# Edge network of a graph kernel: block parts copied one step later, and four groups' sums gathered in one PSUM bank

## The chip, the cores and the metric

The kernel runs on one core of one Trainium2 chip. The metric is the device time of one execution, in microseconds. Engines are named as in the profile: PE (TensorE; PEld is its weight loading), DVE (VectorE), ACT (ScalarE), POOL (GpSimd) and SP (SyncE, which here only issues transfers).

## The reference

12,500 nodes with 96 features, 400,000 edges sorted by destination, 32 attributes an edge. The edge network, the part that the change touches, computes for each edge a message and a gate and sums their products by destination:

```python
edge_input = jnp.concatenate([x[src], edge_attr], axis=-1)
messages = _gelu(edge_input @ mW1 + mb1) @ mW2 + mb2
gates = jax.nn.sigmoid(_gelu(edge_input @ gW1 + gb1) @ gW2 + gb2)
aggregated = jax.ops.segment_sum(messages * gates, dst, num_segments=x.shape[0])
combined = jnp.concatenate([x, aggregated], axis=-1)
update = _gelu(combined @ uW1 + ub1) @ uW2 + ub2
```

A layer norm follows, and then two graph convolutions, each a sum over the same edges weighted by edge weight and degrees, with a gated mix of old and new features:

```python
msg = norm[:, None] * h[row]
out = jax.ops.segment_sum(msg, col, num_segments=n)
g = jax.nn.sigmoid(h_in @ Wr + br)
x = jax.nn.relu((1.0 - g) * h_in + g * xc)
```

## The kernel before, in words

The edges lie in tiles of 128. Four tiles are a quad, two quads a group, two groups (four quads, 2,048 edges) an iteration of the edge network; there are 196 iterations and 392 groups. `edge_pass` runs them on every engine in step: 4 iterations that prepare (`prepare`), then 192 that also build (`pair`, two iterations in a loop body). Each engine follows its own written order, and semaphores couple them. The four steps s = 0 to 3 of an iteration are the four quads:

- POOL (`gather`) fetches the source rows of a quad with four indirect transfers into `hid[s]`, as soon as the quad four places earlier has been weighed (`s_gated`). An iteration needs 16 gathers.
- PE (`edges`) at step s multiplies the attributes of the quad three places ahead (`attr_product`), builds block part 2s (`build_part`, twelve bf16 matmuls into one of the three banks of `part_bank`), waits for the quad's weighed messages and sums them by destination with four matmuls (L1149), and builds part 2s + 1.
- DVE (`edges`) at step s makes the one-hot matrix and the gate column (`gate`), adds a finished window of sums to `acc` (`window_sum`, at s = 0 and s = 2), makes one-hot operands for the block parts (`spread_sides`, L1700 to L1703), multiplies and reduces the gate's logits of the next quad (`dot`), and adds attributes to gathered rows two quads ahead (`add`).
- ACT (`edges`) at step s weighs the messages of the quad by the gate (`weigh`, L1352, four activations, after which `s_gated` rises), copies part 2s from PSUM to `blocks` (`keep_part`, L1361), does the tanh of the next quad and the gelu of the one after it, and copies part 2s + 1.

A group's sums cover 64 destinations (`WINDOW`), in columns of bank `sg[0]`, one half for each of the iteration's two groups. `window_sum` reads the group's first destination from `base_i` and adds 98 rows by 64 columns to `acc` there; it waits for PE's sums of the group's second quad (`s_seg`), and PE starts the next sums of that half only after it (`s_acc`). `hot` and `msg` have two buffers each, so `gate` of a quad waits for PE's sums of the quad two before. The block parts take three banks in turn: `build_part(i)` waits until the part that was in its bank has been copied (`bank_free`, `s_evac`). `spread_sides` at s = 2 overwrites operands of parts 0 to 3 and waits until part 3 is built; at s = 0 it does so for parts 4 to 7 of the iteration before.

The blocks, adjacency matrices of the last 1,536 tiles, go to DRAM and feed the convolutions, whose code the change leaves alone.

Of the kernel before, what the change touches and what calls it, by code (L numbers as in the profile page):

```python
# [20 lines left out]
I32 = mybir.dt.int32  # L21
# [3 lines left out]
AX = mybir.AxisListType  # L25
# [26 lines left out]
ACC = NODES + WINDOW  # L52
# [6 lines left out]
SETUP_STEPS = 21  # L59
# [112 lines left out]
def build(nc, io):  # L172
    ctx = contextlib.ExitStack()
    with ctx:
# [34 lines left out]
        with contextlib.ExitStack() as edges_phase:  # L209
# [8 lines left out]
            iota_z = sb_in(edges_phase, "iota_z", [P, 2 * Z_PAD], F16)  # L218
        table_sb = sb("table_sb", [P, BLOCKS * D])
# [149 lines left out]
        sums = [sg[0][:, WINDOW * g:WINDOW * (g + 1)] for g in range(GROUPS_PER_ITER)]  # L369
# [207 lines left out]
        def edge_pass(eng, rounds, iteration, round_end=None, part=None, round_start=None, alone=0, end=None):  # L577
# [3 lines left out]
            with eng.Fori(0, rounds) as r:  # L581
                n0 = eng.snap(r * ITERS)
                o0 = eng.snap(r * OCTETS)
                w0 = eng.snap(r * OCTET_PAIRS)

                def prepare(c, ahead):
                    done = eng.snap(r * SLICES + c)
                    if part:
                        part(c, done)
                    iteration(c, n0 + c, isinstance(c, int) and c == 0, False, None, ahead)  # L590
                    if end:
                        end(c, done)

                def pair(w, final):
                    for h in range(2):
# [4 lines left out]
                                  None if last else (o + 1, eng.snap(o0 + o + 1)))  # L600
# [3 lines left out]
                prepare(0, None)  # L604
                with eng.Fori(1, SLICES - 1) as c:
                    prepare(c, None)
                prepare(SLICES - 1, (0, o0))
# [42 lines left out]
        def _(sp):  # L650
# [47 lines left out]
            def edges(it, n, first, last, build, ahead):  # L698
# [205 lines left out]
        def _(pool):  # L904
# [43 lines left out]
            def gather(it, n, first, last, build, ahead):  # L948
# [12 lines left out]
            def gather_end(r):  # L961
                wait_apart(pool, s_acc, r * GROUPS + GROUPS)
# [75 lines left out]
        def _(pe):  # L1038
# [64 lines left out]

            def load_places(nb):
# [26 lines left out]
            def edges(it, n, first, last, build, ahead):  # L1131
# [6 lines left out]
                for s in range(QUADS_PER_ITER):  # L1138
# [7 lines left out]
                    if s % 2 == 0 and not (first and s == 0):  # L1146
                        pe.wait_ge(s_acc, GROUPS_PER_ITER * n + s // 2)
# [8 lines left out]
            def edges_end(r):  # L1156
                pe.wait_ge(s_acc, r * GROUPS + GROUPS)
# [131 lines left out]
        def _(act):  # L1289
# [65 lines left out]
            def keep_part(i, nb, h, w):  # L1355
                q, b = divmod(i, QUAD_PARTS)
# [9 lines left out]
            def edges(it, n, first, last, build, ahead):  # L1366
# [4 lines left out]
                for s in range(QUADS_PER_ITER):  # L1371
                    weigh(n, s)
                    if build:
                        keep_part(2 * s, *build[1:])
# [8 lines left out]
                    if build:  # L1383
                        keep_part(2 * s + 1, *build[1:])
# [17 lines left out]
            edge_pass(act, rounds, edges, lambda r: act.wait_ge(s_acc, r * GROUPS + GROUPS),  # L1402
# [102 lines left out]
        def _(dve):  # L1505
# [76 lines left out]
            do.did(v.tensor_scalar(top[:, 1:2], top[:, 0:1], 0.0, None, ALU.max))  # L1582
# [15 lines left out]

            def add_window(it, n, g, rows, first, s_sum, value, s_done):

                start = dve.value_load(base_i[0:1, bass.ds(it * GROUPS_PER_ITER + g, 1)], min_val=0, max_val=NODES)
                window = acc[0:rows, bass.ds(start, WINDOW)]
                if not first:
                    dve.wait_ge(s_done, GROUPS_PER_ITER * n + g)
                dve.wait_ge(s_sum, value)
                v.tensor_tensor(window, window, sums[g][0:rows, :], ALU.add).then_inc(s_done, 1)  # L1606
# [101 lines left out]
            def window_sum(it, n, g, first):  # L1708
                add_window(it, n, g, ACC_ROWS, first, s_seg, QUADS_PER_ITER * n + 2 * g + 2, s_acc)
# [438 lines left out]
```

## Time and profile before

| | |
|---|---|
| median of 3 runs | 10818.27 us (10817.15 to 10834.14) |
| profiled execution, its own time | 10833.28 us |
| its span | 10831.3 us |
| edge network, first to last add to `acc` | 163.5 to 5712.1 us |
| what follows it (node update, two convolutions) | to the span's end |

The profiled execution lies 15 us above the median, and 2 us of its time lie outside the span. Lines of a timeline give the start in us, the duration in us, the engine, the line of the kernel, the operation with output and inputs, how many instructions the line merges (x8), and in brackets the idle time of the engine before it with what ended it. "remote" there is a semaphore whose raiser the profile does not name. The starts and ends of matmuls are PE's own records and their ends are modelled; when another engine gets to see a matmul's semaphore can only be read from that engine's own row.

### The profile page before, as it was taken

The page shows a single profiled execution, that of the slowest core. Times are in us where ns is not written, and L with a number is a line of the kernel's source. Part 1 is how long each engine was busy: PE and PEld are TensorE (multiplying, and loading weights), DVE is VectorE, ACT ScalarE, POOL GpSimd, SP SyncE. Part 2 cuts the span into 40 slices and gives each one's busy share as a digit, 9 for nine tenths or more (in the row PEclk, how much of TensorE's full clock was granted, in tenths as well). Part 3 has the DMA queues.
Part 4 walks back from the last instruction along what each step waited for, and adds up shares of the span by engine and source line. Part 5 has one row for each costly group of instructions (what it writes and reads, how often), then busy time and mean ns, then how long its engine had stood idle before and what let it go on. Part 6 is the DMA issues. An engine that isn't in the chain of part 4 may idle for free. (4 is left out here: it accounts for less than half of the span.)

```text
span 10831.3 us, 151063 instructions
## 1 busy us (share of the span) xinstructions
PE 8115.2 (75%) x42144; PEld 5216.6 (48%) x42144; DVE 4910.5 (45%) x11836; ACT 2686.7 (25%) x6600; POOL 6404.8 (59%) x6424
## 2 busy tenths in 40 slices
PE   4777777777777777777777577787777578877876
PEld 3555555555555555555554333343334333333333
DVE  7666666666666666666666122222222122222222
ACT  3444444444444444444443000000000000000000
POOL 4555555555555555555555666666664666666664
PEclk7888888888888888888887788888887688888887
DMA  4444444444444444444444466666665466665656
GB/s 148 128 137 137 134 140 132 139 132 139 132 138 135 136 138 133 139 132 139 131 139 152 144 212 215 207 228 209 211 214 200 157 208 223 216 220 200 222 207 213
DMA packets 936184, 1818.04 MB, mean 168 GB/s; under 512 B 280495, under 2 KB 748736, under 8 KB 878448
## 3 DMA queue, kind: packets, MB, share of 16 engines
q10 hardware_dynamic: 65600, 773.65, 18.9%
q1 hardware_dynamic: 618592, 578.41, 16.9%
q0 software_dynamic: 251856, 464.10, 16.1%
q8 instruction: 93, 1.52, 0.1%
q14 instruction: 43, 0.35, 0.0%
HBM read 1361.12 MB, written 454.48 MB: 168 GB/s over the span
## 5 line engine op out<-in xcount | busy, mean ns | idle before, releaser
L956 POOL DMA_INDIRECT hid<-src_table,src_ids x3127 | 3121.3, 998 | 2450.0 <-ACT msg L1352 1514.8
L1234 PE MATMUL bd<-ring,table_sb 128*96 128x480 f32 x6272 | 2898.5, 610 | 382.7 <-issue 381.5
L1234 PEld LDWEIGHTS bd<-ring,table_sb 128*96 128x96 f32 x6272 | 1070.0, 175 | 1954.7 <-issue 1954.7
L1001 POOL DMA_INDIRECT hid<-conv_table,hid x1596 | 1552.2, 973 | 715.1 <-issue 488.4
L1149 PE MATMUL sg<-hot,msg 128*98 128x64 f32 x6272 | 817.2, 283 | 1256.1 <-ACT msg L1352 1256.1
L1149 PEld LDWEIGHTS sg<-hot,msg 128*98 128x98 f32 x6272 | 733.3, 196 | 1379.3 <-issue 1303.6
L1001 POOL DMA_INDIRECT feat_in<-conv_table,hid x1056 | 1022.6, 968 | 588.6 <-issue 342.8
L1126 PE MATMUL bd<-one_hot_dst,one_hot_src 128*128 128x168 bf16 (+1 forms) x10368 | 1246.2, 275 | 88.5 <-issue 87.6
L1966 DVE TENSOR_TENSOR acc<-acc,sg 96x64 f32 x400 | 87.3, 218 | 2365.6 <-remote 1368.1
L1361 ACT ACTIVATE blocks<-bd 128x480 f32<-128x480 f32 (+1 forms) x1152 | 657.8, 571 | 1971.7 <-PE bd L1126 941.6
L1126 PEld LDWEIGHTS bd<-one_hot_dst,one_hot_src 128*128 128x128 bf16 x10368 | 1013.5, 110 | 108.6 <-issue 94.3
L1703 DVE SCALAR_TENSOR_TENSOR one_hot_src<-iota_lo,side_now 128x384 bf16<-128x384 bf16 x1536 | 933.0, 607 | 0.0
L1352 ACT ACTIVATE msg<-hid,msg 128x96 f32<-128x96 f32 x3136 | 909.8, 363 | 46.5 <-DVE msg L1680 46.5
L1093 PE MATMUL pa<-w_attr,attr 128*128 128x384 f32 x1568 | 815.5, 656 | 57.1 <-DVE hid L1656 26.9
L1606 DVE TENSOR_TENSOR acc<-acc,sg 98x64 f32 x392 | 86.9, 222 | 1430.5 <-remote 1363.5
L1459 ACT ACTIVATE buf_b<-pa,mix_b_half 96x448 f32<-96x448 f32 x56 | 35.2, 629 | 2817.9 <-PE pa L1243 1635.9
L1339 ACT ACTIVATE hid<-hid 128x768 f32<-128x768 f32 x784 | 656.9, 838 | 279.1 <-DVE hid L1656 223.9
L1001 POOL DMA_INDIRECT rows_more<-conv_table,hid x528 | 525.0, 994 | 293.5 <-issue 157.3
L1093 PE MATMUL pb<-w_attr,attr 128*128 128x384 f32 x1568 | 596.4, 503 | 9.0 <-issue 9.0
L1944 DVE TENSOR_TENSOR conv_hot<-iota_now,hid 128x512 f32<-128x512 f32 x134 | 92.5, 691 | 1019.7 <-remote 581.9
L1093 PEld LDWEIGHTS pa<-w_attr,attr 128*128 128x128 f32 x1568 | 394.6, 279 | 263.6 <-issue 160.5
L1473 ACT ACTIVATE hid<-bd,side_flag 96x480 f32<-96x480 f32 x32 | 21.0, 657 | 1884.6 <-PE bd L1234 893.4
(248 smaller groups left out, 10323.9 us busy)
## 6 DMA issues: line engine op xcount, KB each, us to landing
ring<-adjacency ACTq DMA_DIRECT2D x448, 1680.0 KB
adjacency<-blocks SPq DMA_DIRECT2D x384, 980.0 KB
attr<-in_attr SPq DMA_DIRECT2D x392, 128.0 KB
hid<-src_table,src_ids POOLq DMA_INDIRECT x3127
hid<-conv_table,hid POOLq DMA_INDIRECT x1596
feat_in<-conv_table,hid POOLq DMA_INDIRECT x1056
conv_table<-table_sb SPq DMA_DIRECT2D x28, 336.0 KB, 2.5
feat_half<-feat_keep SPq DMA_DIRECT2D x56, 168.0 KB
```

Source lines behind the costliest of these rows:

```text
L956: pool.indirect_dma_start(out=hid[s][:, t, :], out_offset=None, in_=src_rows, in_offset=bass.IndirectOffsetOnAxis(ap=src_ids[s // 2][:, j: ...
L1001: pool.indirect_dma_start(out=conv_g[j][slot][:, t, :], out_offset=None, in_=conv_rows[l], in_offset=bass.IndirectOffsetOnAxis(ap=conv_ids ...
L1093: last = nc.tensor.matmul(attr_ps[s % 2][:, 512 * h:512 * h + 2 * H2], attr[s // 2][:, P * (s % 2):P * (s % 2 + 1)], w_attr[:, 2 * H2 * h: ...
L1126: op = nc.tensor.matmul(out[:, :, bass.ds(places[q][t], FAN)], y_s[q][t][:, k, :], z_s[q][t][:, z0:z0 + FAN * m].rearrange("p (b d) -> p b ...
L1149: op = nc.tensor.matmul(sums[s // 2][0:ACC_ROWS, :], msg[s % 2][:, t, :], hot[s % 2][:, t, :], start=(s % 2 == 0 and t == 0), stop=(s % 2 ...
L1234: op = nc.tensor.matmul(side_ps[w].rearrange("r (o z) -> r o z", o=UNIT_OCTETS), table_sb[:, D * k:D * (k + 1)], ring[slot][:, :, OCTET_FA ...
L1339: nc.scalar.activation(flat, flat, ACT.Gelu).then_inc(s_gelu, 1)
L1352: op = nc.scalar.activation(m[:, t, 0:D], hid[s][:, t, 0:D], ACT.Copy, scale=m[:, t, GATE_ROW:GATE_ROW + 1])
L1361: nc.scalar.activation(blocks[h][:, first:first + m, WIDTH * q:WIDTH * (q + 1)], part_bank[i % BANKS][:, 0:WIDTH * m].rearrange("p (b w) - ...
L1703: v.scalar_tensor_tensor(out=y_s[q][t][:, :, :], in0=iota_lo[:, :].unsqueeze(1).to_broadcast([P, 3, P]), scalar=side_now[:, 0, QUAD * q + ...
L1944: v.tensor_tensor(conv_s[j][slot], iota_now[:, :].unsqueeze(1).to_broadcast([P, GROUP, WINDOW]), conv_rel[j][:, cols].unsqueeze(2).to_broa ...
L1966: v.tensor_tensor(window, window, sg[j][0:D, WINDOW * slot:WINDOW * (slot + 1)], ALU.add).then_inc(s["acc"], 1)
```

## The change

It has two parts.

**Copies a step later (ACT).** `keep_part` at step s copies parts 2s - 2 and 2s - 1 in place of 2s and 2s + 1; at s = 0 these are the last two parts of the iteration before. Banks, waits of PE and sizes stay.

**One sum for four groups (PE, DVE).** Two iterations (four groups) form a span. A span has a first destination (`span_base`), each group an offset in it of 0 to 96 (`offset_i`), limited there, with what exceeds it taken into the group's own positions. PE reads the two offsets of an iteration into registers, clears 160 columns of `sg[0]` at the start of a span with one matmul of zeros after DVE has added the span before, and lets all 32 matmuls of the span add at their register offset. DVE adds 98 by 160 to `acc` once a span (`span_sum`), at s = 0 of the next span's first iteration, behind `add`. The two `window_sum` of each iteration go. The preparing iterations are written out instead of looped, and the setup has seven more small DVE steps on 128 by 392 values.

```diff
+                if half == 0 and s == 0:
+                    if not first:
+                        pe.wait_ge(s_acc, span)
+                    nc.tensor.matmul(sums, zero[:, :].to_broadcast([P, ACC_ROWS]), first_base[:, 0:SPAN], start=True, stop=False)
                     for t in range(QUAD):
-                        op = nc.tensor.matmul(sums[s // 2][0:ACC_ROWS, :], msg[s % 2][:, t, :],
-                                              hot[s % 2][:, t, :], start=(s % 2 == 0 and t == 0),
-                                              stop=(s % 2 == 1 and t == QUAD - 1))
+                        op = nc.tensor.matmul(sg[0][0:ACC_ROWS, bass.ds(offset[s // 2], WINDOW)], msg[s % 2][:, t, :],
+                                              hot[s % 2][:, t, :], start=False,
+                                              stop=(half == SPAN_ITERS - 1 and s == QUADS_PER_ITER - 1 and t == QUAD - 1))
...
                 for s in range(QUADS_PER_ITER):
                     weigh(n, s)
-                    if build:
-                        keep_part(2 * s, *build[1:])
+                    behind = build and not (s == 0 and isinstance(build[0], int) and build[0] == 0)
+                    if behind:
+                        keep_part(2 * s - 2, *build[1:])
                     if s + 1 < QUADS_PER_ITER:
                         tanh(n, s + 1, not (first and s == 0))
...
-                    if build:
-                        keep_part(2 * s + 1, *build[1:])
+                    if behind:
+                        keep_part(2 * s - 1, *build[1:])
+                if last:
+                    for i in (PARTS - 2, PARTS - 1):
+                        keep_part(i, *build[1:])
...
-            def window_sum(it, n, g, first):
-                add_window(it, n, g, ACC_ROWS, first, s_seg, QUADS_PER_ITER * n + 2 * g + 2, s_acc)
-
-            def edges(it, n, first, last, build, ahead):
+            def span_sum(it, n, span):
+
+                start = dve.value_load(span_i[0:1, bass.ds(it // SPAN_ITERS, 1)], min_val=0, max_val=N)
+                total = acc[0:ACC_ROWS, bass.ds(start, SPAN)]
+                after(dve, s_acc, span)
+                dve.wait_ge(s_seg, QUADS_PER_ITER * (n + SPAN_ITERS))
+                v.tensor_tensor(total, total, sums, ALU.add).then_inc(s_acc, 1)
...
                     gate(it, n, s, not (first and s < 2))
-                    if s == 0 and not first:
-                        window_sum(it - 1, n - 1, 1, False)
-                    if s == 2:
-                        window_sum(it, n, 0, first)
...
+                    if s == 0 and half == 0 and not first:
+                        span_sum(it - SPAN_ITERS, n - SPAN_ITERS, span - 1)
                 if last:
-                    window_sum(it, n, 1, False)
+                    span_sum(it - (SPAN_ITERS - 1), n - (SPAN_ITERS - 1), span)
...
+            def load_offsets(it):
+                _, offsets = nc.values_load_multi_w_load_instructions(
+                    offset_i[0:1, bass.ds(it * GROUPS_PER_ITER, GROUPS_PER_ITER)], engines=[mybir.EngineType.PE],
+                    min_val=0, max_val=LAST_OFFSET, skip_runtime_bounds_check_because="DVE has bounded them")
+                return offsets
```

The order of instructions at three places shows it. First ACT, step 0 of a building iteration, before:

```order
L1352 ACTIVATE msg<-hid,msg 128x96 [waits gate_columns]
L1352 ACTIVATE msg<-hid,msg 128x96 x3
L1358 ISA
L1359 ISA [waits blocks_kept0]
L1361 ACTIVATE blocks<-bd 128x24x20 [waits block_built]
L1342 REGISTER_ALU
L1345 ACTIVATE buf_h<-buf_h,gate_b_half 128x4 [waits gated,gate_logits]
L1337 REGISTER_ALU
L1339 ACTIVATE hid<-hid 128x768 [waits added]
```

and the same place now:

```order
L1370 ACTIVATE msg<-hid,msg 128x96 [waits gate_columns]
L1370 ACTIVATE msg<-hid,msg 128x96 x3
L1380 ISA
L1382 ACTIVATE blocks<-bd 128x24x20 [waits block_built]
L1360 REGISTER_ALU
L1363 ACTIVATE buf_h<-buf_h,gate_b_half 128x4 [waits gated,gate_logits]
L1355 REGISTER_ALU
L1357 ACTIVATE hid<-hid 128x768 [waits added]
```

The rows read alike, but the copy (L1361, now L1382) behind the weighing is that of part 6 of the iteration before, where it was part 0 of this one; the wait for the stored blocks has moved on with part 0 to step 1. Next DVE at the start of an iteration that is the first of its span, from the gate to the operands of the block parts, before:

```order
L1678 COPY msg<-weight 128x4
L1679 REGISTER_ALU
L1680 TENSOR_SCALAR msg<-buf_h 128x4 [waits tanh_done]
L1601 ISA
L1601 TENSOR_LOAD base_i
L1601 ISA x2
L1604 ISA
L1605 ISA [waits accumulated]
L1606 ISA [waits segment_sums]
L1606 TENSOR_TENSOR acc<-acc,sg 98x64
L1696 ISA
L1700 TENSOR_SCALAR one_hot_wide<-iota_wide,side_now 128x1960 [waits block_built]
```

and now, from the end of the same gate to the add to `acc`:

```order
L1712 TENSOR_SCALAR msg<-buf_h 128x4 [waits tanh_done]
L1728 ISA
L1732 TENSOR_SCALAR one_hot_wide<-iota_wide,side_now 128x1960 [waits block_built]
...
L1697 TENSOR_TENSOR prod<-hid,gate_w 128x384 [waits gate_logits,gelu_done]
L1700 TENSOR_REDUCE buf_h<-prod 128x4 [waits gate_products]
L1685 ISA
L1686 REGISTER_ALU [waits gathered2]
L1688 TENSOR_TENSOR hid<-pa,hid 128x768 [waits attr_product]
L1742 ISA
L1742 TENSOR_LOAD span_i
L1742 ISA x2
L145 ISA
L1746 ISA [waits segment_sums,accumulated]
L1746 TENSOR_TENSOR acc<-acc,sg 98x160
```

The wait for PE's sums (`segment_sums`) no longer stands between the gate and the operands; the operands' own wait for the parts (`block_built`, L1700, now L1732) is the next one there. Last PE at the sums of the same step, before:

```order
L1126 MATMUL bd<-one_hot_dst,one_hot_src 128x24x7 x3
L1145 REGISTER_ALU
L1147 REGISTER_ALU [waits gated]
L1149 MATMUL sg<-hot,msg 98x64 [waits accumulated]
L1149 MATMUL sg<-hot,msg 98x64 x3
L1115 REGISTER_ALU
L1120 MATMUL bd<-one_hot_wide,one_hot_src 128x500 [waits block_copied]
```

and now:

```order
L1141 MATMUL bd<-one_hot_dst,one_hot_src 128x24x7 x3
L1161 REGISTER_ALU
L1164 REGISTER_ALU [waits gated]
L1165 MATMUL sg<-first_base,zero 98x160 [waits accumulated]
L1167 ISA
L1167 MATMUL sg<-hot,msg 98x64 x4
L1130 REGISTER_ALU
L1135 MATMUL bd<-one_hot_wide,one_hot_src 128x500 [waits block_copied]
```

The wait for DVE's add has moved to the matmul of zeros, which stands there in every second iteration; at the other steps the sums wait for the weighing alone.

## Rows read from the trace of the kernel before

**Rows 1.** Edge network as one stretch: busy PE, PEld, DVE, ACT, POOL, granted clock, DMA

```profile
330.00:5720.00 5390.00, 4088.61 (x27394) 3119.51 (x27392) 3438.55 (x8549) 2414.32 (x6089) 3022.66 (x3031) 0.86 0.45 136
```

**Rows 2.** The line L1606, all of the program

```profile
L1606 DVE TENSOR_TENSOR acc<-acc,sg x392: 207/222/225, 163.5 to 5712.1; 98x64 f32 x196
```

**Rows 3.** Who waited for whom, 600 to 5600 us: total, times, longest

```profile
DVE acc L1606 <- remote: 1274.8, 329, 5.3
...
PE sg L1149 <- ACT msg L1352: 1110.0, 352, 5.9
ACT blocks L1361 <- PE bd L1126: 888.2, 337, 5.1
ACT blocks L1361 <- remote: 799.5, 178, 6.2
```

**Rows 4.** Timeline of one half iteration, 3033.9 to 3047.9 us

```profile
3033.95 0.90 PE L1149 MATMUL sg<-hot,msg 128*98 128x64 f32 x8 [2.14 <-ACT msg L1352]
...
3034.62 1.05 POOL L956 DMA_INDIRECT hid<-src_table,src_ids  x1 [3.72 <-ACT msg L1352]
...
3038.13 0.99 PE L1126 MATMUL sg<-one_hot_dst,one_hot_src 128*128 128x168 bf16 x9
...
3038.95 0.84 PE L1149 MATMUL sg<-hot,msg 128*98 128x64 f32 x8
...
3039.16 0.57 ACT L1361 ACTIVATE blocks<-sg 128x480 f32<-128x480 f32 x1 [0.44 <-PE sg L1126]
...
3040.01 1.02 PE L1126 MATMUL bd<-one_hot_dst,one_hot_src 128*128 128x175 bf16 x9
...
3043.79 0.94 POOL L956 DMA_INDIRECT hid<-src_table,src_ids  x1 [0.30 <-issue]
3044.81 0.22 DVE L1606 TENSOR_TENSOR acc<-acc,sg 98x64 f32 x1 [3.72 <-remote]
3046.16 0.59 ACT L1361 ACTIVATE blocks<-bd 128x500 f32<-128x500 f32 x1 [4.90 <-remote]
3046.16 0.73 DVE L1700 TENSOR_SCALAR one_hot_wide<-iota_wide,side_now 128x1960 bf16<-128x1960 f16 x1 [1.13 <-remote]
...
3047.93 1.59 PE L1149 MATMUL sg<-hot,msg 128*98 128x64 f32 x8 [4.41 <-ACT msg L1352]
```

**Rows 5.** Two half iterations side by side, busy time and granted clock

```profile
3019.90:3032.10 12.20, 11.90 (x72) 8.94 (x72) 7.08 (x18) 4.59 (x11) 8.13 (x8) 0.75 0.27 75
3033.90:3046.10 12.20, 9.30 (x72) 7.13 (x72) 7.34 (x21) 4.64 (x11) 7.98 (x8) 1.00 0.75 240
```

**Rows 6.** Groups of instructions, 600 to 5600 us: busy, mean ns, idle before

```profile
L956 POOL DMA_INDIRECT hid<-src_table,src_ids x2823 | 2815.8, 997 | 2182.2 <-ACT msg L1352 1364.0 <-issue 818.2
...
L1703 DVE SCALAR_TENSOR_TENSOR one_hot_src<-iota_lo,side_now 128x384 bf16<-128x384 bf16 x1411 | 857.0, 607 | 0.0
...
L1352 ACT ACTIVATE msg<-hid,msg 128x96 f32<-128x96 f32 x2824 | 819.3, 363 | 0.0
...
L1361 ACT ACTIVATE blocks<-bd 128x500 f32<-128x500 f32 (+1 forms) x1059 | 604.7, 571 | 1799.3 <-PE bd L1126 872.2 <-remote 789.3 <-issue 137.1
L1339 ACT ACTIVATE hid<-hid 128x768 f32<-128x768 f32 x706 | 591.6, 838 | 205.1 <-DVE hid L1656 204.2 <-issue 0.4
...
L1702 DVE TENSOR_SCALAR one_hot_dst<-iota_z,side_now 128x688 bf16<-128x688 f16 x1059 | 422.3, 399 | 0.0
...
L1668 DVE TENSOR_REDUCE buf_h<-prod 128x4 f32<-128x384 f32 x705 | 389.9, 553 | 24.2
L1665 DVE TENSOR_TENSOR prod<-hid,gate_w 128x384 f32<-128x384 f32 x705 | 386.4, 548 | 0.0
...
L1656 DVE TENSOR_TENSOR hid<-pa,hid 128x768 f32<-128x768 f32 x352 | 333.6, 948 | 0.0
L1676 DVE TENSOR_TENSOR hot<-iota_now,rel 128x256 f32<-128x256 f32 x705 | 291.3, 413 | 0.0
```

**Rows 7.** Register load of the block places, PE's sequencer, all of the program

```profile
L1106 PEldq TENSOR_LOAD <-side_off x192: 813/817/850, 272.3 to 5690.7; - x192
```

More of the change, by code:

```diff
@@ L51 @@
 WINDOW_LOG2 = 6
-ACC = NODES + WINDOW
+SPAN_ITERS = 2
+SPANS = ITERS // SPAN_ITERS
+SPAN_GROUPS = GROUPS // SPANS
+LAST_OFFSET = 96
+SPAN = LAST_OFFSET + WINDOW
+ACC = N + SPAN
 GATE_ROW = D
@@ L368, in build @@
         iota, gate_w2_now = iota_now[:, :], gate_w2[:, :]
-        sums = [sg[0][:, WINDOW * g:WINDOW * (g + 1)] for g in range(GROUPS_PER_ITER)]
+        sums = sg[0][0:ACC_ROWS, 0:SPAN]
         part_bank = [px, const, sg[1]]
@@ L589, in prepare @@
                         part(c, done)
-                    iteration(c, n0 + c, isinstance(c, int) and c == 0, False, None, ahead)
+                    iteration(c, n0 + c, c == 0, False, None, ahead, c % SPAN_ITERS, s0 + c // SPAN_ITERS)
                     if end:
@@ L599, in pair @@
                         iteration(it, n0 + it, False, last, (o, eng.snap(o0 + o), h, eng.snap(w0 + w)),
-                                  None if last else (o + 1, eng.snap(o0 + o + 1)))
+                                  None if last else (o + 1, eng.snap(o0 + o + 1)), h,
+                                  eng.snap(s0 + w + BUILD_FROM // SPAN_ITERS))
                 if round_start:
                     round_start(r)
[L604 to L607, printed above, removed]
+                for c in range(SLICES):
+                    prepare(c, (0, o0) if c == SLICES - 1 else None)
                 for w in range(alone):
@@ L696, in store_blocks, with edges @@
                              kept[:, i, :, :]).then_inc(s_block_out[h], 16)
-            def edges(it, n, first, last, build, ahead):
+            def edges(it, n, first, last, build, ahead, half, span):
                 for b in range(GROUPS_PER_ITER):
@@ L946, in _, with gather @@
                 pool.wait_ge(s_table_out[p], 16 * (CHUNKS // 2))
-            def gather(it, n, first, last, build, ahead):
+            def gather(it, n, first, last, build, ahead, half, span):
                 for s in range(QUADS_PER_ITER):
@@ L1129, in build_part, with edges @@
                 op.then_inc(s_built, 1)
-            def edges(it, n, first, last, build, ahead):
+            def edges(it, n, first, last, build, ahead, half, span):
+                offset = load_offsets(it)
                 if build:
@@ L1364, in keep_part, with edges @@
                     ACT.Copy).then_inc(s_evac, 1)
-            def edges(it, n, first, last, build, ahead):
+            def edges(it, n, first, last, build, ahead, half, span):
                 if first:
@@ L1597, in _ @@
             new_source(CHUNKS - 1, (CHUNKS - 1) % 2)
[L1599 to L1606, printed above, removed]
             def place_windows(do, slots, shift, flag):
@@ L1706, in spread_sides, with edges @@
                                            op0=ALU.is_equal, op1=ALU.mult).then_inc(s_yz, 1)
-            def window_sum(it, n, g, first):
-                add_window(it, n, g, ACC_ROWS, first, s_seg, QUADS_PER_ITER * n + 2 * g + 2, s_acc)
-            def edges(it, n, first, last, build, ahead):
+            def span_sum(it, n, span):
[4 more added lines that the diff above has]
+                v.tensor_tensor(total, total, sums, ALU.add).then_inc(s_acc, 1)
+            def edges(it, n, first, last, build, ahead, half, span):
                 if first:
```

43 lines of the change are left out of this document (35 added, 8 removed).

## The prediction

> **What bounds the kernel now.** I read the busy shares first. Over 5,390 us of the edge network no engine is full: PE 76%, DVE 64%, POOL 56%, ACT 45% [rows 1]. So something makes them take turns. From the first to the last add to `acc` 5548.6 us pass [rows 2], 28.3 us for each of 196 iterations. The groups of instructions give POOL's share of that: a gather takes 997 ns, and with the issue gaps (818.2 us over 2,823) one starts each 1.29 us [rows 6], 20.6 us for sixteen. POOL is idle the other 7.7 us, for the weighing of messages: in the same row of [rows 6] 1364.0 us are put down to ACT. The chain of waits would name two lines as guilty, DVE's add to `acc` (1274.8 us, 329 times) and ACT's copies of block parts (888.2 + 799.5 us), while PE's sums wait 1110.0 us for ACT [rows 3].
>
> The timeline shows what stands behind them. In the half iteration of [rows 4] PE sums a quad at 3033.95, POOL starts eight gathers at 3034.62 and starts the last at 3043.79. PE's sums of the second quad are recorded as ended at 3039.79 (3038.95 + 0.84), yet the DVE add that waits for them starts at 3044.81. Block part 3 ends at 3041.03 in PE's record, yet ACT's copy and DVE's L1700 that wait for it both start at 3046.16. Then come the copy, the weighing (L1352) and PE's next sums at 3047.93. Early in the run of gathers it is otherwise: the part that ends at 3039.12 is copied from 3039.16. So a matmul's end is seen at once in about the first 5 us of a run of gathers, and after that only when the run is over, here 2.4 us after the last gather started. I can't say why; I only take the rule. PE's own speed doesn't set it: one half iteration with 11.90 us of PE work at clock 0.75, and the next with 9.30 us at 1.00, are both 14 us long [rows 5].
>
> A half iteration then adds up to 0.7 (sums to first gather) + 7 x 1.29 + 2.4 (release) + 0.6 (copy) + 1.2 (four times 363 ns [rows 6]) = 13.9 us. Two make 27.8 where 28.3 are measured, so the sum is 2% short. The engines stop for each other twice an iteration.
>
> **The span sums.** The 392 adds of 222 ns [rows 2] go, 87 us of DVE's time; 98 adds of 160 columns come. Their price lies between the 0.22 of 64 columns and the 0.55 of a 384-column operation [rows 6]; I take 0.32, so 31 us. Both lie in DVE's slack, and count only in a chain through DVE. But the wait of this add isn't worth its 1,275 us: behind it stands L1700 with its own wait for part 3, and in [rows 4] that costs 1.13 us more. Gone alone, the first wait becomes the second, at the same moment. PE's 98 matmuls of zeros are each about one sum of the `sg` kind (0.11 us in [rows 4], 0.90 for eight) up to 0.4: at most 40 us, behind POOL's stop, so nothing. PE also loads two offsets an iteration: one load of the block places takes 0.82 us [rows 7], so 196 x 0.82 = 160 us if it stood in the open. It stands at the head of an iteration, ahead of a product that PE has early enough (PE idles 1110.0 us for weighing [rows 3]); I take nothing. Seven DVE steps of setup on 392 values: up to 0.55 each [rows 6], 4 us with their waits; I take 3.
>
> **The copies a step later.** Before, the weighing of quads 0 and 2 is followed by the copy of a part that PE is just building, and what lies behind it on ACT (tanh, gelu, the next copy, the next weighing) waits too. Now the parts copied are long built, and the next quad can be weighed without that stop. PE pays for it: it can't build part i + 3 until part i is copied, so it waits for ACT where ACT waited for it.
>
> I laid out one iteration from the moment when held matmuls are seen, with the durations of [rows 6] (operands of an even step L1700 0.73 [rows 4], L1702 0.40 and twice L1703 0.61: 2.35; of an odd step 2.0; dot 1.1; add 0.95; gate 0.41 and two small steps: 0.8). Gate a ends at 0.8, copy 0.6, weighing a 2.0. POOL does four gathers, the first from 2.7 to the last at 6.6. PE finishes its part, sums, builds on to 2.6. DVE: operands, dot, add, gate b at 7.8. ACT: tanh, gelu (0.84), copy, weighing b 9.7. POOL, dry since 7.9, restarts at 10.3; this is the one pause within an iteration. DVE goes on, gate c 12.6; ACT weighs c to 14.4. Part work that ended at 11.7 is seen at once, 1.4 us into the new run. Gate d 17.8 (18.2 with the span sum), weighing d 19.6. Gate a' of the next iteration needs PE's sums of quad c; those can only run after part 0', which waited for a copy until 15.0, and so at 16.2 to 17.1, more than 6 us into POOL's run. They are held. POOL's twelve gathers last start at 10.3 + 11 x 1.29 = 24.5; release at 26.9.
>
> So 26.9 us by my layout, one stop in place of two. Its kin for the kernel before gave 27.8 against 28.3 measured, 0.25 us for each stop; with one I take 27.1. **The sum:** 192 x (27.1 - 28.3) = -230; setup +3; 10,833 - 230 + 3 = 10,606. Slack in the layout is on the side of gain (gate d and weighing d are done 5 us before the gathers end, and held work can be seen earlier when gathers stand apart), about 0.2 us of an iteration, -40: 10,565 for a profiled execution. That of before lies 15 us above its median, so 10,550.
>
> **Rivals.**
> (A) One stop per iteration, as above: 10,550; its own range 10,300 to 10,750, 0.7 us of an iteration less or 1.0 more for the pause within it. Chance 0.50.
> (B) No hold at all. If the quads flow, the runs of gathers break up and matmuls are seen in time. Then POOL's 20.6 us bind, with DVE's 18 us (3438.55 of 5,390 us, times 28.3) close below. At 22 us an iteration the gain is 6.3 x 192 = 1,210: 9,610. For it: early in a run matmuls are seen at once [rows 4]. Against it: a run without pauses is just where they were held. Chance 0.10. The notes that bear on it are the Trainium skill, "SBUF — State Buffer", section "SBUF: two separate sides": a DVE operation in a two-port mode locks GpSimd out, and it can't write its descriptors meanwhile. The trace agrees only in part: a gather beside a busy DVE takes 1.05 us at 3034.62 and 0.94 at 3043.79 beside an idle one [rows 4], 997 in the mean [rows 6]. Were each of the 3.9 us of L1700 and L1702 an iteration to stop POOL in full, case B would be 16 x 1.24 + 3.9 = 23.7 us and 9,950 in place of 9,610; A would not change.
> (C) The stop only moves to L1700, which waits for part 3 (then for part 7) as before, and weighing stays tied to it. 28.3 us stay: about 10,820, the same. For it: both start at 3046.16 [rows 4]. Against it: the copies are off ACT's way, and L1700 comes after gate and weighing. Chance 0.10.
> (D) Slower. If ACT's late copies hold part 0' until the weighing of quad a is at 3.5 in place of 2.0, POOL's four gathers last start at 8.1 and end at 9.3, and the next quad is there by about then: POOL has no pause, and the fresh 5 us in which matmuls are seen never come. PE's part of about 11 us, which L1700 of quad c waits for, is then held until POOL does run dry: eight gathers to 4.2 + 7 x 1.29 = 13.2, more if quads weighed ahead prolong the run. Laid out in the same way, I get six quads in 45.4 us, 30.3 an iteration: +2.0 x 192 = +384, 11,200. It decides if the pause at 7.9 to 10.3 (2.4 us) is eaten up. For it: PE waits for copies that ACT does a step later, with three banks only, and ACT idled 1,688 us for parts before [rows 3]. Against it: the copies themselves are ready at once. Chance 0.30.
>
> **From the cases to the numbers.** About 0.2% (22 us) is what a measurement of this kernel tells from no change. A falls on the side of faster, B too; C within; D slower: faster 0.60, same 0.10, slower 0.30. The range reaches from between A and B (9,750, which takes in B's slower form) to just short of D's value, 11,150, leaving out 2 in 10. A's own is 10,300 to 10,750.
>
> **What the changed profile would show.** The `acc` line 98 times, near 0.3 us, hardly waiting; 27.1 us between the first gathers of iterations; POOL's wait for L1370 once in an iteration of 2.4 us and once of about 3.9, gathers in runs of four and twelve; ACT's copies with little idle time, and PE's parts waiting for them in its place. Case B would show runs of gathers with gaps under 1 us and DVE over 80% busy; C the idle time of L1606 back at L1732; D one run of 20 or more gathers and DVE idle for 5 us or more before L1732. I am wrong if a matmul's end is held by something other than the run of gathers, or if the order of copies ties PE to ACT in a place that my layout misses; the clock can't do it, since both of its levels gave the same period [rows 5].

## Result and the profile after

The changed kernel takes 11,534.57 us in the median of four runs (11470.42 to 11643.47), the kernel before 10,818.1: ratio 1.0635 [1.0584, 1.0685]. It is slower. The slowest of the four runs, 11,643.47 us, counts as a slow one and is left out of the ratio. Here and below a ratio is the one on record, with its 95% interval; it can lie up to 0.3% off the quotient of the two medians. The prediction said 10,550 us, with a range up to 11,150. The profiled execution has a span of 11,469.0 us, 638 more than before.

The place is plain from the adds to `acc`. The first row gives count, durations and the first and last start of the line's instructions, the second who waited for them:

```profile
L1746 DVE TENSOR_TENSOR acc<-acc,sg x98: 309/311/322, 234.4 to 6361.0; 98x160 f32 x98
...
  PE sg L1165: 391.1, 85
```

The add itself came as costed (98 times, 0.311 us where 0.32 was taken; it waited once for PE's sums, 4.9 us). But the edge network ends at 6361.3 in place of 5712.1 [rows 2]: 649 us, 3.4 us for each of 192 iterations. What follows the edge network lost nothing (5,108 us, 5,119 before).

Who waited for whom, 600 to 5600 us (total, times, longest):

```profile
POOL hid L965 <- ACT msg L1370: 1802.9, 325, 8.9
ACT buf_h L1363 <- DVE buf_h L1700: 1791.6, 500, 10.7
DVE one_hot_wide L1732 <- remote: 1287.4, 153, 9.9
...
DVE one_hot_wide L1732 <- PE bd L1141: 557.3, 134, 9.8
...
PE bd L1135 <- ACT blocks L1382: 333.0, 63, 7.7
...
PE sg L1165 <- DVE acc L1746: 301.6, 69, 7.7
```

and POOL's gathers as a group (busy, mean ns, idle before):

```profile
L965 POOL DMA_INDIRECT hid<-src_table,src_ids x2525 | 2496.4, 989 | 2504.3 <-ACT msg L1370 1802.9 <-issue 697.1 <-DMA src_ids<-in_src 4.3
```

A gather costs the same 0.99 us. Busy and idle time together over 2,525 gathers, times 16, give 31.7 us an iteration; the same row of before gives 28.3 [rows 6]. POOL's wait for weighed messages rose from 7.7 to 11.4 us an iteration. The 1,275 us that DVE waited at L1606 [rows 3] are back, and more, at L1732 (1287.4 + 557.3), and ACT, which used to wait for parts, waits 1791.6 us for the dot. The timeline shows the order of it:

```profile
3036.18 1.16 ACT L1370 ACTIVATE msg<-hid,msg 128x96 f32<-128x96 f32 x4
...
3038.15 0.95 POOL L965 DMA_INDIRECT hid<-src_table,src_ids  x1 [3.60 <-ACT msg L1370]
...
3040.25 1.16 ACT L1370 ACTIVATE msg<-hid,msg 128x96 f32<-128x96 f32 x4
...
3042.94 0.94 PE L1141 MATMUL bd<-one_hot_dst,one_hot_src 128*128 128x175 bf16 x9
...
3046.97 0.95 POOL L965 DMA_INDIRECT hid<-src_table,src_ids  x1 [0.30 <-issue]
...
3049.57 0.73 DVE L1732 TENSOR_SCALAR one_hot_wide<-iota_wide,side_now 128x1960 bf16<-128x1960 f16 x1 [9.87 <-remote]
...
3051.59 0.55 DVE L1697 TENSOR_TENSOR prod<-hid,gate_w 128x384 f32<-128x384 f32 x1
3052.17 0.55 DVE L1700 TENSOR_REDUCE buf_h<-prod 128x4 f32<-128x384 f32 x1
...
3052.76 0.30 ACT L1363 ACTIVATE buf_h<-buf_h,gate_b_half 128x4 f32<-128x4 f32 x1 [9.80 <-DVE buf_h L1700]
...
3054.37 0.57 ACT L1382 ACTIVATE blocks<-bd 128x500 f32<-128x500 f32 x1
...
3054.84 1.16 ACT L1370 ACTIVATE msg<-hid,msg 128x96 f32<-128x96 f32 x4
...
3056.81 0.95 POOL L965 DMA_INDIRECT hid<-src_table,src_ids  x1 [8.89 <-ACT msg L1370]
```

Part 3 ends at 3043.88 in PE's record, 5.7 us into POOL's run, and DVE sees it at 3049.57, when the run is over. The trace's own events of PE's semaphores agree: those of part 3, of the next attribute product and of part 4, whose recorded ends are 3043.88, 3045.19 and 3046.34, lie between 3049.55 and 3049.73. I call this late sight of PE's ends the hold. So far it is as before. New is what comes between that and the next gather: operands, dot, tanh, gate, a copy and the weighing, 7.24 us to the gather. [rows 4] have 1.8 us from 3046.16 to PE's next sums, and a gather follows 0.7 us behind those: 2.4 us. Before, the weighing that came behind the hold was of a quad whose gate was made already; ACT had been kept from it by the copy of part 3. Now ACT has weighed that quad at 3040.25, early, and the next one needs the dot that stands on DVE behind the waiting operands. POOL stands still for 8.89 us in place of 3.72.

This is the worst kind of stop, and not every one is of it. From 600 to 5600 us POOL stops for over 1 us 338 times, 2.1 times an iteration, mostly for 2 to 9 us. L1732 starts within 114 of these stops, with 7.24 us (median) from its start to the next gather. In others it is released while the run still goes on, and the chain behind it outlasts the run, here by 5.82 us:

```profile
3065.38 0.73 DVE L1732 TENSOR_SCALAR one_hot_wide<-iota_wide,side_now 128x1960 bf16<-128x1960 f16 x1 [7.23 <-remote]
...
3072.75 0.95 POOL L965 DMA_INDIRECT hid<-src_table,src_ids  x1 [5.82 <-ACT msg L1370]
```

Of the runs of gathers between the stops 189 are of eight, 53 of twelve and 50 of four. Two runs of eight in a row, an iteration's gathers, take 33.8 us from start to start of the next run; a run of four and one of twelve take 28.4.

### The profile page after: what moved, and what is told of

Same layout as the page of the kernel before. It is cut to its first block and busy times, and to the rows that moved or that the text cites. A ratio compares the mean times of both kernels' runs of the same rounds, so it can differ in the third digit from the quotient of the medians.

```text
span 11469.0 us, 149487 instructions
## 1 busy us (share of the span) xinstructions
PE 8246.6 (72%) x42340; PEld 5241.8 (46%) x42341; DVE 4814.2 (42%) x11551; ACT 2672.9 (23%) x6600; POOL 6382.1 (56%) x6424
## 5 line engine op out<-in xcount | busy, mean ns | idle before, releaser
L1141 PE MATMUL bd<-one_hot_dst,one_hot_src 128*128 128x168 bf16 (+1 forms) x10368 | 1281.2, 285 | 3.3 <-issue 3.3
L1732 DVE TENSOR_SCALAR one_hot_wide<-iota_wide,side_now 128x1960 bf16<-128x1960 f16 x384 | 284.8, 742 | 2293.0 <-remote 1581.7
L1141 PEld LDWEIGHTS bd<-one_hot_dst,one_hot_src 128*128 128x128 bf16 x10368 | 1076.4, 115 | 19.6 <-issue 1.8
L1167 PE MATMUL sg<-hot,msg 128*98 128x64 f32 x6272 | 784.8, 270 | 160.7 <-issue 128.4
L1363 ACT ACTIVATE buf_h<-buf_h,gate_b_half 128x4 f32<-128x4 f32 x784 | 232.6, 297 | 2662.1 <-DVE buf_h L1700 2157.8
L1135 PE MATMUL bd<-one_hot_wide,one_hot_src 128*128 128x480 bf16 (+1 forms) x1152 | 496.9, 431 | 488.2 <-ACT blocks L1382 417.4
L1382 ACT ACTIVATE blocks<-bd 128x480 f32<-128x480 f32 (+1 forms) x1152 | 647.5, 562 | 465.6 <-remote 441.3
L1102 PE MATMUL pb<-w_attr,attr 128*128 128x384 f32 x1568 | 625.2, 523 | 75.9 <-issue 70.6
L1102 PEld LDWEIGHTS pa<-w_attr,attr 128*128 128x128 f32 x1568 | 367.9, 260 | 626.4 <-DVE hid L1688 420.5
```

The lines of the kernel that those rows point to most:

```text
L1102: last = nc.tensor.matmul(attr_ps[s % 2][:, 512 * h:512 * h + 2 * H2], attr[s // 2][:, P * (s % 2):P * (s % 2 + 1)], w_attr[:, 2 * H2 * h: ...
L1135: nc.tensor.matmul(flat, y_s[q][0][:, 0, :], wide, start=True, stop=False)
L1141: op = nc.tensor.matmul(out[:, :, bass.ds(places[q][t], FAN)], y_s[q][t][:, k, :], z_s[q][t][:, z0:z0 + FAN * m].rearrange("p (b d) -> p b ...
L1167: op = nc.tensor.matmul(sg[0][0:ACC_ROWS, bass.ds(offset[s // 2], WINDOW)], msg[s % 2][:, t, :], hot[s % 2][:, t, :], start=False, stop=(h ...
L1382: nc.scalar.activation(blocks[h][:, first:first + m, WIDTH * q:WIDTH * (q + 1)], part_bank[i % BANKS][:, 0:WIDTH * m].rearrange("p (b w) - ...
L1732: v.tensor_scalar(z_wide[q][:, :], iota_wide[:, :], place, None, ALU.is_equal)
```

## The experiments

The runs fell on several chips, and the kernel before was run beside each set. It took 10,938 us in the first set (chip 12 of the record), 10,824 in the second (chip 9), and 8,866, 8,859, 8,862 and 8,860 us in the last four (chips 7, 3, 9 and 2). Chip 9 stands with both levels, half an hour apart. So if the numbers name the same chips throughout, the level is not a property of the chip; what sets it is not known. The sets of 10,800 to 10,940 us are called those with the hold, the others those without it. Ratios are compared, and only where the kernel before is alike.

**First set (before: 10,937.93 us). One part at a time, and the dot moved.** Kernels are named by the first letters of their labels. `e1` is the kernel before with ACT's order of the changed one (no span sums); `e2` is the changed kernel with

```
                     weigh(n, s)
...
-                    if behind:
-                        keep_part(2 * s - 2, *build[1:])
+                    if build:
+                        keep_part(2 * s, *build[1:])
```

and 2s + 1 at the second place. `e3` is the changed kernel, and `e4` the kernel before, with

```
-                    if s < 2 and build:
-                        spread_sides(1, 2 * s, build[1])
-                    if s >= 2 and ahead:
-                        spread_sides(0, 2 * (s - 2), ahead[1])
+                    if s % 2 == 1:
+                        if s < 2 and build:
+                            spread_sides(1, 2 * s, build[1])
+                        if s >= 2 and ahead:
+                            spread_sides(0, 2 * (s - 2), ahead[1])
                     if s + 1 < QUADS_PER_ITER:
                         dot(n, s + 1, False)
...
+                    if s % 2 == 0:
+                        if s < 2 and build:
+                            spread_sides(1, 2 * s, build[1])
+                        if s >= 2 and ahead:
+                            spread_sides(0, 2 * (s - 2), ahead[1])
                     if s + 2 < QUADS_PER_ITER:
                         add(it, n, s + 2)
```

so that at steps 0 and 2 the dot is ahead of the operands that wait for parts, and the add is still behind them.

> The kernel before with the copies a step later and nothing else. Theory 1 (the copies): before, ACT's weighing stood behind the copy of part 3 or 7, so when held matmuls were seen only a copy and a weighing (1.8 us) lay before the next gathers. With late copies the weighing has run ahead, and after the hold DVE's whole chain (operands 2.0, dot 1.1, tanh 0.3, gate 0.6, copy 0.5, weighing 1.2, start of the gather 0.7, together 7.2 us) lies bare. Then this kernel alone carries nearly all the loss: 11,350 to 11,550 us, ratio 1.05 to 1.065. Theory 2 (the matmul of zeros waits for DVE's add of the span, 391 us in the changed kernel): nothing of that is in here, so 10,820 us, or up to 1% off.

Measured: 11,834.32 us, ratio 1.0851 [1.0786, 1.0915]. The late copies alone carry the whole loss, and more than theory 1 said. Its waits look like those of the changed kernel, with more of PE's for the copies:

```profile
ACT buf_h L1345 <- DVE buf_h L1675: 2051.6, 499, 11.8
POOL hid L956 <- ACT msg L1352: 1993.8, 306, 9.4
DVE acc L1613 <- remote: 899.0, 129, 10.1
...
PE bd L1120 <- ACT blocks L1364: 825.2, 133, 9.4
DVE one_hot_wide L1707 <- remote: 715.5, 198, 6.9
```

Theory 2 is no longer needed for the loss: there are no zeros in this kernel.

> The changed kernel with the copies back at their old step: span sums alone. Theory 1: the old chain behind the hold is back, the zeros find DVE's add done or nearly; 10,750 to 10,850 us, ratio 0.995 to 1.003. Theory 2: over 11,100 us.

Measured: 10,999.12 us, ratio 1.0061 [1.0044, 1.0078]. Span sums alone cost 0.6%, a little outside what theory 1 gave and far from theory 2. The two parts are not additive: beside the late copies the span sums seem to win 1.4 to 2.2% back (1.0709 below and 1.0635 against 1.0851, but on different chips).

> The changed kernel, but at the even steps DVE does the dot of the next quad ahead of the operands that wait for the block parts. Theory 1: the chain behind the hold is 1.1 us (dot) and some of the tanh shorter at each of two holds in an iteration: 2 x 1.1 x 192 = 420 us less than 11,470, so 11,000 to 11,100 us. A third theory (PE's waits for part banks, 333 us, set the period): no change, 11,450 to 11,550.

Measured: 11,575.81 us, ratio 1.0595 [1.0556, 1.0635]. The chain behind L1732 did get shorter: from its start to POOL's next gather 6.18 us in place of 7.24 (medians over the stops in which L1732 starts), the 1.06 us of the dot. But the ratio lies 0.4 points below the first measurement of the changed kernel, which its interval does not tell from nothing, and 1.1 below the second; both of these are from other sets. Some 3.7% were expected. ACT now waits for the add, which is still behind the operands:

```profile
ACT hid L1357 <- DVE hid L1688: 2146.9, 539, 11.8
POOL hid L965 <- ACT msg L1370: 1844.9, 312, 8.4
DVE one_hot_wide L1732 <- remote: 1557.0, 199, 9.7
```

So the bare chain is there, but its length is no simple term of the period. The shorter chain stands bare more often: L1732 starts within 173 of 326 stops of POOL, where in the changed kernel it did within 114 of 338. POOL's wait did not fall (1844.9 us, 1802.9 in the changed kernel). Theory 1 has the right place and too simple a sum.

> The kernel before with the same move of the dot. There the weighing behind the hold does not need the dot, so theory 1 expects 10,800 to 10,840 us, ratio 0.998 to 1.002. If the dot counted in the kernel before as well (then the 7.2 us chain is no new thing of the change), it would be 200 us or more faster.

Measured: 10,964.46 us, ratio 1.0025 [1.0012, 1.0037], about what was expected and not faster: the dot is no part of the chain behind the hold in the kernel before.

**Second set (before: 10,824.3 us). Both copies early, the changed kernel again, and fewer or smaller gathers.** `e5`:

```
                         keep_part(2 * s - 2, *build[1:])
+                        keep_part(2 * s - 1, *build[1:])
                     if s + 1 < QUADS_PER_ITER:
                         tanh(n, s + 1, not (first and s == 0))
...
-                    if behind:
-                        keep_part(2 * s - 1, *build[1:])
```

> The changed kernel, but at step s both copies (parts 2s - 2 and 2s - 1) stand directly behind the weighing, ahead of tanh and gelu. Theory 4: in the changed kernel the second copy stands behind tanh and gelu, these behind DVE's dot and add, these behind operands that wait for the hold; so PE gets the bank of part 2s + 1 late (5.15 us idle before L1135 in one place), builds part 3 some 5 us later, more than 5 us into POOL's run, and its end is held: another bare chain of 7.2 us. With both copies early PE is not late, part 3 is seen at once, and at least one long stop of 8.7 us in an iteration shrinks by 3 us or more: 3 x 192 = 576 us or more off, ratio to before 1.01 or less. If instead the copies' place does not matter (the bare chain is there whatever PE does), the ratio stays 1.05 to 1.065.

> The changed kernel as it is, on this chip, for comparison with the others of this set: ratio 1.055 to 1.07.

Measured: `e5` 11,572.55 us, ratio 1.0709 [1.0677, 1.0742]; `e6` 11,581.34 us, ratio 1.0709 [1.0681, 1.0737]. No difference, and theory 4 falls. The timeline of `e5` tells why:

```profile
3031.24 0.95 POOL L965 DMA_INDIRECT hid<-src_table,src_ids  x1 [3.85 <-ACT msg L1370]
...
3033.84 0.97 PE L1141 MATMUL bd<-one_hot_dst,one_hot_src 128*128 128x175 bf16 x9
...
3037.07 0.84 PE L1167 MATMUL sg<-hot,msg 128*98 128x64 f32 x8
...
3039.79 0.59 ACT L1382 ACTIVATE blocks<-bd 128x500 f32<-128x500 f32 x1 [4.68 <-remote]
3039.79 0.73 DVE L1731 TENSOR_SCALAR one_hot_wide<-iota_wide,side_now 128x1960 bf16<-128x1960 f16 x1 [6.35 <-remote]
3040.02 1.32 POOL L965 DMA_INDIRECT hid<-src_table,src_ids  x1 [0.30 <-issue]
```

PE is early as theory 4 wanted: part 3 ends at 3034.81, 3.6 us into POOL's run. It is held nevertheless, until 3039.79, and this time not until the run is over: the last gather starts at 3040.02. My "first 5 us of a run are free, then all is held to its end" was too simple at both ends.

`e7` leaves out half of the gathers after the first iteration (`range(QUAD_SPARED[s] if first else QUAD // 2, QUAD)`, and the semaphore counts to match), `e8` half of the rows of each (`hid[s][0:64, t, :]`, ids of 64 partitions). Both leave half of the source rows out of the sums.

> The kernel before with two gathers a quad in place of four after the first iteration (half of the source rows are left out of the sums). If PE's ends are held by POOL's run of gathers and released with it, the runs are 4 long, the hold ends about 2.4 us after the last start or does not happen, and a half iteration takes 0.7 + 3 x 1.29 + 2.4 + 1.8 = 8.8 us, or what DVE needs, 9 us, in place of 14: edge network about 5549 - 192 x 10 = 3,630 us. If the hold is PE's own (its time to build and sum), the edge network stays above 5,000 us.

> The kernel before with all gathers, but each fetches 64 rows in place of 128 after the first iteration (half of the source rows are left out). If the hold follows POOL's instructions, their count and time decide: if a gather still takes near 1 us, period 26 to 28.3 us an iteration. If it follows the rows in flight (descriptors, bytes), ends are seen at once for more of the run and the last wait for a part ends before the last gather does: period below 24 us.

Measured, one run each: `e7` 8,980.28 us, `e8` 10,866.65 us. The busy times of `e7` from 330 to 3870 us (PE, PEld, DVE, ACT, POOL, clock):

```profile
330.00:3870.00 3540.00, 3422.36 (x27058) 2621.85 (x27055) 3326.32 (x8453) 2452.97 (x6012) 1446.71 (x1500) 1.00 0.54 163
```

1,500 gathers in 3,540 us, 8 an iteration: 18.9 us, with PE 97% busy. The work of PE, DVE and ACT is what it was, so 28.3 us was never their limit. The longest wait for a part is short now (600 to 3600 us: total, times, longest):

```profile
DVE one_hot_wide L1700 <- PE bd L1126: 124.9, 259, 1.1
```

The hold is not gone altogether: of the 620 parts that end 1 to 2 us into a run (600 to 3600 us) 313 raise their semaphore late, by 0.7 us in the median and 1.4 at most. In `e8` the group of gathers reads

```profile
L957 POOL DMA_INDIRECT hid<-src_table,src_ids x2797 | 2685.7, 960 | 2317.4 <-ACT msg L1353 1407.5 <-issue 909.9
```

A gather of 64 rows takes nearly as long, and (2685.7 + 2317.4) / 2,797 x 16 = 28.6 us an iteration remain. So the hold follows POOL's instructions or their time, and not the rows in flight; this rests on one run each.

**Last sets (before: 8,866, 8,859, 8,862, 8,860 us). A gap in POOL's run.** POOL writes a scratch tile and waits for itself ahead of a quad's gathers:

```
+                    if not first and s in (0, 1, 2, 3):
+                        for k in range(2):
+                            pool.memset(idle[:, :], 0.0).then_inc(s_idle, 1)
+                            wait_apart(pool, s_idle, 8 * (n - 1) + 2 * (0, 1, 2, 3).index(s) + k + 1)
```

(`e9`, `f2`, `g2`); in `e11`, `f3` and `g3` four of them at s = 1 and 3; in `e10` one ahead of every gather; in `e12` four very small ones at each step of the changed kernel.

> The kernel before, with POOL kept busy by two small memsets of its own (about 0.8 us together) before the four gathers of every quad. Theory 5: what holds PE's ends is POOL's unbroken run of gathers; a gap in it lets them through. Then the add to acc, the copy of part 3 and L1700 start before the run of eight is over, and an iteration gets shorter than 28.3 us although POOL has 3 us more to do: 25 to 27 us, 10,200 to 10,600 us. If the hold is bound to something else (time since the run began, rows in flight), the pauses only add: 28.3 plus 1.6 to 3 us, 11,100 to 11,400 us.

> The same with one memset (about 0.4 us) before every gather. Theory 5 with short gaps enough: period 24 to 27 us. If a gap has to be longer than 0.7 us to let PE through: 28.3 + 16 x 0.4 = 34.7 us at most, over 11,300 us.

> The same with four memsets (about 1.6 us) in the middle of each run of eight only. Theory 5: matmuls that ended by 6 us are seen in the gap; part 3 (ends at 7 to 8 us) is not held more than before: period 26 to 29 us. Else 28.3 + 3.2 = 31.5 us, 11,440 us.

> The changed kernel with four very small memsets (0.5 to 1 us together) before each quad's gathers. Theory 5: L1732 no longer waits for the end of the run, the bare chain of 7.2 us starts earlier, and the time falls below 11,000 us. Else it rises by 2 to 4 us an iteration, to 11,900 us or more.

Measured: 1.139 [1.1351, 1.1428], 11,792.63 us (1.33), 9,864.76 us (1.11), 1.1193 [1.1155, 1.1232]. They say nothing for or against theory 5, for here the kernel before takes 8,866 us and has no hold to break. Where POOL itself is the limit, a pause adds its time.

> The changed kernel as it is. On a chip on which the kernel before takes about 10,820 us (PE's ends are held late in a run of gathers): ratio 1.055 to 1.075. On one on which it takes about 8,866 us (there no end of a matmul was held in the four traces taken): the theory that the whole loss comes through the hold expects a ratio of 0.99 to 1.02; a loss of 5% there too would mean that the copies cost their time without any hold.

> The kernel before with POOL kept busy by two memsets before each quad's gathers. On a chip with the hold: theory 5 (a gap in POOL's run lets PE's ends through) expects 25 to 27 us an iteration, ratio 0.94 to 0.98; if gaps do not matter, 28.3 plus 1.6 to 3, ratio 1.03 to 1.06. On a chip without the hold: 1.139 as measured.

> The same with four memsets in the middle of each run of eight. With the hold, theory 5: ratio 0.93 to 1.00, and the add to acc is no longer seen only after the run. If gaps do not matter: 1.04 to 1.06. On a chip without the hold: 1.11 as measured.

Measured, again without the hold: `f1` 8,893.2 us, ratio 1.0031 [1.0007, 1.0055]; `f2` 1.1371 [1.1338, 1.1404]; `f3` 1.1132 [1.11, 1.1165]. The first is the most telling number of the study: where nothing is held, the change that costs 6 to 7% elsewhere costs 0.3%.

> The kernel before as it is, for its trace on this chip. On a chip where it takes about 8,860 us: L1606 and L1700 wait for parts or sums hardly at all (under 0.5 us each), POOL has no stops of 3.5 us, an iteration takes 21 to 22 us. On one where it takes about 10,820 us: the same picture as in the first trace, 28.3 us.

> The kernel before with two memsets of POOL before each quad's gathers. On a chip with the hold, theory 5 (gaps in POOL's run let PE's ends through) expects ratio 0.94 to 0.98; if gaps do not matter, 1.03 to 1.06. On a chip without the hold 1.137, as measured twice.

> The kernel before with four memsets in the middle of each run of eight gathers. On a chip with the hold, theory 5 (a gap lets PE's ends through): sums and part 3 are seen in the gap, POOL finds the next quad weighed, 26.6 us an iteration, ratio 0.95 to 0.98. If gaps do not matter: 28.3 + 2 x 1.5 to 3, ratio 1.05 or more. On a chip without the hold 1.113, as measured twice.

Measured: `g1` 8,867.74 us, `g2` 1.1382 [1.1349, 1.1415], `g3` 1.1117 [1.1085, 1.115]. The trace of `g1` is the kernel before where nothing is held: of 2,228 ends of PE's products, sums and parts between 600 and 3600 us, 2,185 raised their semaphore within 0.3 us, one was late, and the others have no record of their own. In `f1` it is 2,173 of 2,213 and none late. Its waits, its gathers, and its add to `acc` with the idle time before it:

```profile
POOL hid L957 <- issue: 682.1, 2238, 0.4
ACT hid L1340 <- DVE hid L1657: 661.5, 548, 3.9
```

```profile
L957 POOL DMA_INDIRECT hid<-src_table,src_ids x2528 | 2630.7, 1041 | 770.5 <-issue 682.1 <-ACT msg L1353 85.6 <-DMA src_ids<-in_src 2.7
```

```profile
L1607 DVE TENSOR_TENSOR acc<-acc,sg x392: 200/222/225, 171.2 to 4416.3; 98x64 f32 x196
...
  issue: 124.6, 139
  PE sg L1150: 21.4, 15
```

DVE's add waits 21.4 us for PE's sums in the whole program, where in [rows 3] it waited 1274.8 us in part of it. POOL waits 85.6 us for weighed messages (600 to 4000 us), 0.5 us an iteration in place of 7.7, and an iteration takes (2630.7 + 770.5) / 2,528 x 16 = 21.5 us: sixteen gathers and nothing else. The changed kernel there:

```profile
L965 POOL DMA_INDIRECT hid<-src_table,src_ids x2512 | 2636.5, 1050 | 765.3 <-issue 702.2 <-ACT msg L1370 55.8 <-DMA src_ids<-in_src 7.3
```

(2636.5 + 765.3) / 2,512 x 16 = 21.7 us. The same rows give 28.3 and 31.7 where the hold is. The granted clock differs too, 0.96 in `g1` from 330 to 4400 us and 0.86 in [rows 1]. It does not make the hold: the held half iteration of [rows 4] had a clock of 1.00 [rows 5], and in `e7`, also at 1.00, ends were still late.

## Why the prediction was wrong

**What bounds it: right in the trace, but not a property of the kernel.** The sum of the half iteration (gathers, 2.4 us to the release, copy, weighing) stands, and so does the reading that the wait for the sums was worth nothing by itself: the same time came back at L1732, and span sums alone (`e2`) gained nothing (ratio 1.0061). The hold is there in the sets of 10,800 to 10,940 us, and follows the number of gathers (`e7`) and not their rows (`e8`). It is absent in the others, where 21.5 us an iteration are left. Two terms need a word. The sum writes 1.2 us for four times 363 ns, which is 1.45; in the timelines a weighing lasts 1.16, so 1.2 stands. And 0.75 in [rows 5] is the mean of a stretch, so those rows compare full clock with a mixture, and not the clock's two levels.

**The step that failed** is in the layout of the changed iteration: "DVE goes on, gate c 12.6", "Part work that ended at 11.7 is seen at once, 1.4 us into the new run". Part 3 ended 5.7 us into the run (3043.88 against 3038.15), where the layout had 1.4, and was seen after the run; and in `e5`, where it ended at 3.6 us, it was held too. The rule behind the step, that an end in the first 5 us of a run is seen at once, was read from one part in [rows 4], and the rest of that trace speaks against it: of the sums that end 3 to 6 us into a run (70 between 600 and 5600 us) none raised its semaphore within 0.3 us, while of the attribute products that end 4 to 5 us in 188 of 194 did. How far the run has gone does not decide alone, and what else does is not known. From this wrong step followed the wrong place of the hold. I let gate a' of the next iteration be the held one, with only gate, copy and weighing behind it (2.7 us to the next gather). The one that is held is L1732, with DVE's operands and dot, ACT's tanh, the gate, a copy and the weighing behind it: 7.24 us. I had POOL wait some 6.5 us an iteration beside its gathers (27.1 - 20.6); by its rows it waits 11.4 for weighed messages.

**Case A's own shape came in part, and gained nothing.** Runs of four and twelve stand in about a third of the iterations, and there an iteration takes 28.4 us where 27.1 was forecast and 28.1 to 28.3 is the time before. The iterations with two runs of eight take 33.8, and they make the loss.

**The rival that came true is D in sign and place, not in mechanism.** DVE idles 9.87 us before L1732, as D said, and PE waits for copies (333.0 us at L1135). But POOL does stop, its runs are mostly of eight and never of twenty, and `e5` shows that PE's lateness for want of a bank is not what decides. The mark of C, the idle time of L1606 back at L1732, is there as well, but the time did not stay. D's 2.0 us an iteration were 3.4. So D, with a chance of 0.30, is no success of its reasoning.

**The terms.** The add of 160 columns (0.32 taken, 0.311 measured), the offsets' loads at nothing and the setup were right or too small to see. The zeros were not covered as I said: PE waited 391.1 us there for DVE's add, because that add stands behind L1732. Yet `e1` has no zeros and loses more, so the loss does not need this wait.

**The copies are the cause** as far as parts go: `e1` alone loses 8.5%, `e2` 0.6%. That they work through the hold is what `f1` says: the same kernel costs 0.3% where nothing is held, and there the work of the other engines fits into 21.7 us, so without the hold the late copies force no longer period than that. It is as strong as the assumption that nothing else which counts differs between the two levels. How the length of the bare chain turns into time is not settled (`e3` took 1.06 us out of it and won a third of what that should bring, or less), and what the hold is stays open. Whether a gap in POOL's run would break it was not shown either way: no such kernel ran in a set that has it.

## What to carry to other kernels

When a late event releases several engines at once, ask what stands bare behind it, and not only how often it comes: work that is let run ahead of the event takes its cover away, and the chain behind becomes the next quad's whole chain. A rule read from one place of a trace ("seen at once in the first 5 us") has to be counted over the whole trace before a layout rests on it, and needs its own rival. Before tuning such waits, time the kernel on several chips and at several times: here the same code took 10,820 and 8,860 us, and the change cost 6 to 7% or 0.3%.

## What the runs showed of the hardware

- The same kernel has two levels of time: 10,818, 10,938 and 10,824 us in the earlier sets, 8,866, 8,859, 8,862 and 8,860 us in the later. The record's chip 9 stands with both. After the edge network the program also differs: 10,831.3 - 5,712.3 = 5,119 us against 8,865.6 - 4,416.5 = 4,449 us in `g1`.
- At the slower level PE's ends reach DVE and ACT up to 5 or 6 us late while POOL issues gathers (3043.88 to 3049.57; 3034.81 to 3039.79). Where both engines wait for the same part they start in the same moment (3039.79 in `e5`, 3046.16 in [rows 4]). With half as many gathers the delay is at most 1.4 us (18.9 us an iteration, PE 97% busy); half the rows a gather leave it (28.6 us an iteration, 28.3 before).
- A gather of 64 rows keeps POOL 0.96 us, one of 128 rows 0.99 to 1.05 by the run, so the rows hardly count.
- A gather of 128 rows lasts 0.95 us while DVE is idle, and 1.22 us in the mean where it overlaps both L1700 and the L1702 behind it (`g1`, L1701 and L1703 there; 176 gathers). It is slowed and does not wait for the whole of these 1.1 us.
